# A four-layer graph network: the first join, two norms and the next projection as one stage of five groups, lookups in the sort over all 128 rows and columns, and layer 1's node sums added up by a product

## The reference, cut to what matters

```python
h = jnp.maximum(_layernorm(x, axis=-1), 0.0)
x = x + _L0_gnn_ref(h, edge_index, edge_attr_18, ...)        # softmax over the edges of each src
h = jnp.maximum(_layernorm(x, axis=-1), 0.0)
x = x + _L1_gnn_ref(h, edge_attr_64, edge_weight, edge_index, ...)
...
def _L1_gnn_ref(x, edge_features, edge_weights, edge_index, ...):
    xn = _layernorm(x, ln1_g, ln1_b)                         # (x - m) * rsqrt(v + eps) * g + b
    q, k, v = (xn @ Wq + bq), (xn @ Wk + bk), (xn @ Wv + bv) # 8 heads of 32
    scores = einsum('ehd,ehd->eh', q[dst], k[src] + ep[:, None, :]) * scale * ew[:, None]
    m = segment_max(scores, dst); ex = exp(scores - m[dst]); s = segment_sum(ex, dst)
    out = segment_sum((ex / s[dst])[:, :, None] * v[src], dst)
    x = x + alpha * (out @ Wo + bo)
    ...                                                      # norm, feed-forward, add
```

## Time and profile before

| | us |
|---|---|
| median of 3 runs | 8586.36 (8586.0 to 8587.62) |
| the profiled execution | 8571.41 |
| its span in the profile | 8569.7 |
| first scatter, second scatter | 305 to 1325, 1370 to 2390 |
| edges0 | 2440 to 3753 |
| combine0, norm1, norm1a, tables1 | 3754 to 4038 |
| edges1 | 4038 to 5420 |
| edges2, edges3 | 6150 to 7215, 7290 to 8420 |

### The profile page before, as it was taken

How to read it: one execution, slowest core, us unless ns; L and a number is a source line. 1 busy time by engine, 2 the same in 40 slices (tenths; PEclk the granted TensorE clock), 3 DMA queues, 4 the chain that set the end, 5 groups by cost and what they waited for, 6 DMA issues and landing times. The chain is left out here.

```text
span 8569.7 us, 143502 instructions
## 1 busy us (share of the span) xinstructions
PE 6613.0 (77%) x33110; PEld 4732.5 (55%) x33111; DVE 5308.7 (62%) x15263; ACT 3576.5 (42%) x10766; POOL 5221.6 (61%) x5120
## 2 busy tenths in 40 slices
PE   7999998999979989974777777667855555667675
PEld 6777775666646666652555555455433344445454
DVE  6677776666657777774999999721122223455556
ACT  3322222333347666632666666223200000777772
POOL 0477776777767777721777777200277775677772
PEclk9655555555589999997999999879877777887887
DMA  7411111111145555532666666200344443444442
GB/s 219 136 17 16 17 17 26 33 33 34 33 106 140 138 136 138 140 61 96 184 175 175 176 178 175 85 11 33 132 108 108 108 108 80 107 110 109 109 108 47
DMA packets 1013468, 849.20 MB, mean 99 GB/s; under 512 B 751678, under 2 KB 841581, under 8 KB 1009339
## 3 DMA queue, kind: packets, MB, share of 16 engines
q0 software_dynamic: 257152, 645.64, 27.7%
q1 hardware_dynamic: 710069, 154.62, 9.1%
q10 hardware_dynamic: 45780, 44.08, 1.5%
HBM read 723.28 MB, written 120.67 MB: 98 GB/s over the span
## 5 line engine op out<-in xcount | busy, mean ns | idle before, releaser
L1120 POOL DMA_INDIRECT edges_kv<-kv,edges_rec x1712 | 1998.4, 1167 | 968.0 <-issue 511.0
L1230 PE MATMUL banks<-edges_kv,edges_hot 128*128 128x288 f32 (+2 forms) x5136 | 1563.8, 455 | 623.3 <-DVE edges_kv L1476 412.9
L1230 PEld LDWEIGHTS banks<-edges_kv,edges_hot 128*128 128x128 f32 x5136 | 1051.9, 215 | 1005.0 <-issue 563.6
L1631 POOL DMA_INDIRECT edges_rows<-rel,edges_rec x856 | 809.3, 945 | 965.2 <-DMA edges_rec<-by_dst_records 710.0
L545 POOL DMA_INDIRECT by_src_records<-sort_by_src_rec,sort_pos_i x808 | 773.9, 958 | 544.2 <-issue 533.2
L1120 POOL DMA_INDIRECT edges_kv<-feat,edges_rec x856 | 829.3, 969 | 270.4 <-issue 253.9
L675 PE MATMUL banks<-sort_table,sort_hot_hi_t 25*128 25x128 f32 x3232 | 952.1, 444 | 52.0 <-DVE sort_junk L616 47.2
L1647 PE MATMUL banks<-edges_rows,edges_hot 128*128 128x256 f32 x1712 | 625.8, 529 | 466.1 <-DMA edges_rows<-rel,edges_rec 449.2
L545 POOL DMA_INDIRECT by_dst_records<-sort_by_dst_rec,sort_pos_i x808 | 773.7, 958 | 288.0 <-issue 250.3
L1465 DVE TENSOR_TENSOR acc<-edges_pair_sums,acc 128x288 f32 (+2 forms) x1284 | 560.6, 437 | 487.0 <-DMA edges_kv<-feat,edges_rec 268.7
L675 PEld LDWEIGHTS banks<-sort_table,sort_hot_hi_t 25*128 25x128 f32 x3232 | 721.5, 307 | 221.2 <-issue 121.1
(11 more groups left out here) (372 smaller groups left out, 12506.6 us busy)
## 6 DMA issues: line engine op xcount, KB each, us to landing
edges_kv<-kv,edges_rec POOLq DMA_INDIRECT x1712
sort_feat<-in_edge_attr_dram SPq DMA_DIRECT2D x100, 256.0 KB, 3.6
rel<-tables_stage SPq DMA_DIRECT2D x25, 1008.0 KB
by_dst_records<-by_dst_blank ACTq DMA_DIRECT2D x1, 17120.0 KB, 54.2
edges_rec<-by_dst_records SPq DMA_DIRECT2D x107, 160.0 KB
edges_rows<-rel,edges_rec POOLq DMA_INDIRECT x856
edges_kv<-feat,edges_rec POOLq DMA_INDIRECT x856
by_src_records<-sort_by_src_rec,sort_pos_i POOLq DMA_INDIRECT x808, 2.1
```

Of the source, the lines that this page charges most:

```text
L1120: pool.indirect_dma_start(kv[:, r, c, 0:koff + DIM], None, tab, bass.IndirectOffsetOnAxis(ap=reci[:, r, c, idx:idx + 1], axis=0)).then_inc ...
L1230: last = pe.matmul(ps[:, 6 + m % 2, 0:OW], hot[:, b % 2, c, :], kv[:, b % BUFS, c, koff:koff + OW], start=(c % 2 == 0), stop=(c % 2 == 1))
L1631: pool.indirect_dma_start(rows[:, b, c, :], None, tab, bass.IndirectOffsetOnAxis(ap=reci[:, b, c, idx:idx + 1], axis=0)).then_inc(gathered ...
```

## The change

Three things are changed.

**Lookups.** In `scatter`, `hot_hi`, its turned copy and the table get 128 columns or rows instead of 25; the additional ones hold zeros, set once by three memsets on GpSimd in the setup block. The matmuls of L642, L670 and L675 become 128 x 128. ACT still copies 25 rows.

**The sums of layer 1** (`kind == 1` alone). Behind the two products of a pair TensorE multiplies the identity with the block of `acc` (126 rows, 272 columns, f32) into the same bank (`with_past`), so that the bank holds the new sum. ACT copies it into `acc` and, from rows 96 to 127, into `pair_sums` for `ends`. DVE's additions are gone. A new semaphore, `acc_kept`, holds TensorE's `with_past` back until ACT has stored the pair before. `summed`, for which GpSimd waits, is now raised by `with_past`. ACT's pair copies are split (0, 1), (2), (3).

**One stage.** combine0, norm1, norm1a and tables1 become `join_and_project`. Its first block, `split_parts`, is the old one, with the first five picks moved behind the scans, and with the loading of weights beside it: gain times weights on GpSimd, offset times weights on TensorE, added into the bias by DVE. Its second block runs at time t the sums of group t, the join and both norms of group t - 1, and the turned products of group t - 2, t from 0 to 6. Picks compare with an iota instead of node numbers that are counted on. ACT now changes between exponentials and square roots in every group.

```diff
@@ scatter
-        hot_hi = ph.sbuf("hot_hi", [P, 2, G, NB], BF16)
+        hot_hi = ph.sbuf("hot_hi", [P, 2, G, P], BF16)
-        hot_hi_t = ph.sbuf("hot_hi_t", [NB, 2, G, P])
+        hot_hi_t = ph.sbuf("hot_hi_t", [P, 2, G, P])
-        table = ph.sbuf("table", [NB, 2, P])
+        table = ph.sbuf("table", [P, 2, P])
...
-                            last = pe.matmul(ps[0:NB, 0, P * c:P * c + P], hot_hi[:, b % 2, 4 * h + c, :], C.ident_b[:],
+                            last = pe.matmul(ps[:, 0, P * c:P * c + P], hot_hi[:, b % 2, 4 * h + c, :], C.ident_b[:],
                                              start=True, stop=True)
...
-                                last = pe.matmul(ps[0:NB, TABLE, 0:P], hot_hi[:, u, c, :], hot_lo[:, u, c, :],
+                                last = pe.matmul(ps[:, TABLE, 0:P], hot_hi[:, u, c, :], hot_lo[:, u, c, :],
                                                  start=False, stop=False, skip_group_check=True)
...
@@ edge_layer, tensor
+                def with_past(j, b, m):
+
+                    n = at(j, b)
+                    block = blocks_of(pe, O, j, b, UNROLL)[m]
+                    if not (first_steps(j, b, 1) and m == 0):
+                        pe.wait_ge(acc_kept, n(PAIRS, m))
+                    pe.matmul(ps[:, 6 + m % 2, 0:OW], C.ident[0:BN, :],
+                              acc[0:BN, bass.ds(block, 1), :].rearrange("p o w -> p (o w)"), start=False, stop=True).then_inc(summed, 1)
...
@@ edge_layer, scalar
+                        if kind == 1:
+                            act.copy(acc[:, bass.ds(blocks[m], 1), :].rearrange("p o w -> p (o w)"), ps[:, 6 + m % 2, 0:OW]
+                                     ).then_inc(acc_kept, 1)
+                            act.copy(pair_sums[ENDS:P, m, :], ps[ENDS:P, 6 + m % 2, 0:OW]).then_inc(sums_copied, 1)
+                            continue
...
@@ join_and_project, second block
+                for b in range(3 * GROUP):
+                    sum_block(pe, C, L, S, b)
+                pe.wait_ge(weights_scaled, 4)
+                for t in range(2, GROUPS + 2):
+                    b0 = GROUP * (t - 2)
+                    turn(b0)
+                    for i in range(GROUP):
+                        if 3 <= t < GROUPS:
+                            sum_block(pe, C, L, S, GROUP * t + i)
+                        if i + 1 < GROUP:
+                            turn(b0 + i + 1)
+                        multiply(b0 + i)
...
+                def pick(t, i):
+                    if t + 1 < GROUPS:
+                        pick_block(dve, C, O, S, GROUP * (t + 1) + i)
+
+                def evacuate(t, i):
...
+                    dve.wait_ge(mult_done, b + 1)
...
+                    dve.tensor_tensor(stage[:, b % 3, :], ps[:, KV_BANK[b % 2], :], bias[:, 0:KV], ALU.add).then_inc(staged, 1)
...
+                    dve.tensor_tensor(x[:, b, :], ps[:, Q_BANK[b % 2], 0:DIM], bias[:, KV:KV + DIM], ALU.add).then_inc(q_kept, 1)
...
@@ the main program
-            combine(nc, C, L, "combine0", acc, x, True)
...
+            join_and_project(nc, C, L, "tables1", acc, x, kv1, x_kept, h_kept, (A["L1_gnn_ln1_g"], A["L1_gnn_ln1_b"]),
+                             [(A[f"L1_gnn_W{c}"], A[f"L1_gnn_b{c}"]) for c in "qkv"], A["L1_gnn_be"], (DIM // H1) ** -0.5, H1)
...
-                layer_norm(nc, C, "norm1", x, h, kept=x_kept)
-                layer_norm(nc, C, "norm1a", h, hn, (A["L1_gnn_ln1_g"], A["L1_gnn_ln1_b"]), relu=False, kept=h_kept)
-                project(nc, C, "tables1", hn, [(A[f"L1_gnn_W{c}"], A[f"L1_gnn_b{c}"]) for c in "qkv"],
```

More of the change, by code:

```diff
@@ L552, in _ @@
                 def _(act):
-                    act.copy(table[:, 0, :], starts[:]).then_inc(table_ready, 1)
+                    act.copy(table[0:NB, 0, :], starts[:]).then_inc(table_ready, 1)
                     beside.scalar_start(act)
@@ L1081, in edge_layer @@
         added = ph.sem("added")
+        acc_kept = ph.sem("acc_kept")
         dve_set = ph.sem("dve_set")
@@ new lines, in members, with group_of, pick_block, sum_block @@
+def members(g):
+    return range(GROUP * g, GROUP * g + GROUP)
+def group_of(g):
+    return slice(GROUP * g, GROUP * g + GROUP)
+def pick_block(dve, C, O, S, b):
+    if b >= PICKS:
+        dve.wait_ge(S.conts_summed, b + 1 - PICKS)
+    dve.scalar_tensor_tensor(out=S.pick[:, b % PICKS], in0=bc(O.cont_key[:], P), scalar=-(1.0 + BN * b),
+                             in1=C.iota[:].unsqueeze(1).to_broadcast([P, TB, P]), op0=ALU.add, op1=ALU.is_equal).then_inc(S.pick_ready, 1)
+def sum_block(pe, C, L, S, b):
+    pe.wait_ge(S.pick_ready, b + 1)
+    if b >= 2:
+        pe.wait_ge(S.far_copied, b - 1)
+    for k in range(TB):
+        for i in range(3):
+            last = pe.matmul(C.psum[:, b % 2, 0:L.out_width + 1], S.pick[:, b % PICKS, k, :], S.parts[:, i, k, :],
+                             start=(k == 0 and i == 0), stop=(k == TB - 1 and i == 2))
+    last.then_inc(S.conts_summed, 1)
```

466 lines of the change are left out of this document (439 added, 27 removed).

## The result

| | before | after |
|---|---|---|
| median | 8586.18 us (8579.67 to 8587.62, 4 runs) | 8520.02 us (8505.47 to 8525.35, 4 runs) |
| ratio | | 0.9923, 95% interval 0.9907 to 0.9939 |
| profiled execution's span | 8569.7 us | 8503.7 us |

What follows compares the result with a forecast made beforehand. GpSimd was taken to bound the scatters, DVE edges1, and no engine was full from combine0 to tables1. The terms gave 8571 - 5 - 61 - 58 = 8447 us, 8462 as a median, range 8395 to 8525.

Steps and rivals of the forecast that it cites:

- rival 2: edges1: the new chain of waits through acc_kept and summed holds the stage, layer 1 sums gain 0; 8523 us, chance 0.11.
- part B: Sums of layer 1 in edges1: moving DVE's additions to TensorE shortens a step from 12.92 to 12.35 us, -61 us.
- What bounds the scatters: First and second scatter: GpSimd sets the pace, 808 scatters by 1.265 us, and TensorE has some 6% of slack.
- -5 for the part: Lookups made 128 wide and deep in the scatters: only GpSimd's waits and the passes' ends can shrink, -5 us.
- rival 4: Scatters: the wide loads stand in TensorE's way, up to +335 us, 8797 us in all; chance 0.06.
- 82 ns: Scatters: cost per wide load on TensorE from which the whole kernel would be slower.
- Part C: combine0 to tables1 made one stage: overlapping engines end it at 3976 instead of 4034, -58 us.
- The long slot: Second block of the one stage: the third time slot, t = 2, is the longest at 40 us.
- the wait for `acc_kept`: edges1: TensorE's identity product waits for ACT to store the pair before; no more than 0.1 us put on it.
- The sign that I had named as wrong: edges1: "ACT acc" as releaser of many identity products would show the forecast for the layer 1 sums wrong.
- GpSimd's term: edges1: fewer DVE operations with two SBUF operands shorten the mean gather from 1.243 to 1.12 us, 11.4 us a step.
- rival 1: edges1: gathers stay at 1.243 us and GpSimd holds the stage, -29 instead of -61 us; 8494 us, chance 0.12.

Runs made afterwards that it cites:

- kept_by_act: The changed kernel with x and h written to DRAM in the one stage from ACT's queue instead of GpSimd's; ratio 0.9896 to the kernel before.

## Why the prediction was right, and where its terms were off

The time, 8520, lies in the range (8395 to 8525), 5 us from its upper end, and the direction was right; the gain is half of the forecast, and the time is outside of what the forecast gave itself (8425 to 8495). It is next to rival 2's 8523, which is chance: that rival had part B at nothing, while B brought 28.5 us and 22 were lost in stages that no rival named. Without these 22 the time would be 8498.

*What bounds the scatters: right, though a sign of being wrong came.* In the first pair the scatters stand 1.27 apart as before, and a TensorE that needs 274 us less changed the passes by -5.8 and +1.9 us (first to last start). Against -5 for the part, -8.6 stand in the trace. GpSimd's waits did not stay below 11 us: in 305 to 1325 they are 15.5 (256.2 less 240.7 of issue), of them 12.2 for `pos_i`, which had been 2.7. The sum "808 scatters by 1.265 make 1022 us, the length of the pass" had taken the stretch for the pass. From first to last scatter it was 1046.6 us, 27 more than 807 of the median distance; the changed kernel's 1040.8 are 14 more than 807 of its own. So the passes did hold some time beyond GpSimd's pace, and what the change took off that paid for the longer scatters. That wide loads cost nothing was right; rival 4 is out. (Its 82 ns used 143 for 0.2% and the gain of B and C; 17 + 61 + 58 are 136, and the limit 80 ns.) That the clock could leave 0.50 I had said, and it did (0.75).

```profile
L551 POOL DMA_INDIRECT by_src_records<-sort_by_src_rec,sort_pos_i x792 | 765.3, 966 | 256.2 <-issue 240.7 <-DVE sort_pos_i L631 12.2 <-DMA sort_by_src_rec<-in_edge_attr_dram 3.0
```

*Part C: right, 51 of 58 us.* The first evacuation came 3832.65, after 12 us of waiting, the last ended at 3975.7 where I had laid out 3976. That the last number agrees is luck: the stage had begun 8.6 us earlier. Its first block took 32 us as laid out, the second 198 (3777.6 to 3975.7) instead of 190, of which 5 are in the last two slots. The long slot is the one that I named (42 us where I had 40), and neither table loads (nine of 1.28 us) nor picks held it; DVE's waits for the products are the longest, 58.4 us.

```profile
3832.65 0.69 DVE L2438 TENSOR_TENSOR tables_stage<-banks,tables_bias 128x512 f32<-128x512 f32 x1 [12.07 <-PE banks L2349]
...
3975.26 0.41 DVE L2440 TENSOR_TENSOR x<-banks,tables_bias 128x256 f32<-128x256 f32 x1
```

*Part B: the mechanism right, the step mis-sized.* The sum had said "all three, TensorE 11.4, GpSimd 11.4, DVE 10.9, allow about 11.5". TensorE took over as the bound, and its 11.4 was about right for its work (11.2 busy); 11.5 for the step was wrong, since I put 0.1 us on the wait for `acc_kept` and the order around it, and it is 0.7. Measured are 11.9. These gaps are new, not old ones that DVE had hidden. The store of the third pair stands behind ACT's eight one-hots, which costs TensorE 0.37. And gaps of issue now stand in front of `expand` (45.9 us from 4030 to 5300, 31 of them in the six steps in which the loop returns), where before TensorE had waited for nothing but DVE (3.4). They stand right behind the new identity products and the loads of block numbers, which I had put at nothing; that the loads cause them isn't shown. The sign that I had named as wrong, "ACT acc" as the releaser of many identity products, came: 49.7 us over the whole stage, about one product a step.

GpSimd's term was right (mean 1.12 forecast, 1.08 measured) but bought nothing, because its waits for TensorE grew from 61.6 to 139.5 us.

So of the 28.5 us little comes from the undisturbed step (11.97 to 11.9, some 7) and most from fewer long ones: of 106 steps 19 were over 14 us, and 6 are, those in which the loop returns. DVE's busy time fell by 94 and not 183 us: 183 are the lengths of the records, and each had overlapped its neighbours by 0.08; the rest of the difference isn't traced. TensorE's waits in front of the products with the query (L1509, now L1545) did not grow, as I had it, but fell from 37.8 to 12.8; DVE waits for TensorE before the running maxima instead (L1480, 65.5). This is a part of what rival 2 described; rival 1, long gathers, didn't come.

*What was in no term:* 22 us behind edges1. Of these 9 are the longer gathers of edges2, whose length of 957 or 960 ns every build with the one stage shows; 12 are in edges3 and open. I had costed the change at nothing wherever it touches no code, and GpSimd's indirect DMAs changed with the build. With the 15 us in the two scatter passes (an estimate, 1616 by 9 ns) it is the largest single cost of the change.

## What to carry to other kernels

When work moves from the fullest engine to the next, add up not only the next one's busy time but the gaps that the new order gives it: the waits for whoever stores its result, and what stands ahead of that store on its engine. On an engine that has become the bound, each of them lengthens the step. A chain of copies that goes through one more engine for each small piece costs its latency each time, even where every engine has room. And look at how long the same instruction takes in the parts that are not changed: in a kernel whose pace is an instruction of 0.95 us issued 5000 times, 10 ns are up to 50 us.

## What the runs showed of the hardware

- GpSimd's indirect DMA of 128 rows took a median of 946, 949, 957 or 960 ns in edges2, and 958, 962, 967 or 971 in the scatters, with the shortest and the longest of edges2 at most 22 ns apart in a trace. A change elsewhere in the program shifted them together by 9 to 11 ns, and the same program in two traces differed by 3 to 4. Moving plain DMAs off its queue changed nothing. The cause is open.
- TensorE's granted clock stood at 0.50 (1.2 GHz throughout) in a stage where it was 94% busy with matmuls of 25 rows or columns among others, at 0.65 with the lookups 128 rows deep, and at 0.69 and 0.75 (between 1.2 and 2.4 GHz) with all of them 128 by 128.
- A gather of edges1 took 0.95 us beside DVE's reduction and 2.03 beside L1499, which reads two operands from SBUF; on average 1.177 to 1.244 us in the five traces with DVE's four additions and 1.076 to 1.154 in six without.
- The kernel before took 8586 us in the first pair and 10,316 to 10,454 on three chips later, one of which gave both 10,439 and 10,319. The kernels run there have the same instruction times as the first pair (DVE's reduction 2.28 us in both) and more idle time marked as issue and as remote. There the changed kernel, unrolled three times as far, ran at 0.9625 of the kernel before and at 0.973 of `kept_by_act` on the same chip (9937.5 of 10,216.6 us), faster than both kernels.
